# Causal attention's scores: two rows summed by TensorE, row 8's products moved to GpSimd, row 9's to VectorE

## The reference, cut to what matters

```
qkv = jnp.einsum('btd,ed->bte', x, Wqkv)
qkv = qkv.reshape(b, t, 3, H, DK).transpose(2, 0, 3, 1, 4)
q, k, v = (qkv[0], qkv[1], qkv[2])
scores = jnp.einsum('bhtd,bhsd->bhts', q, k) * SCALE
scores = jnp.clip(scores, -10.0, 10.0)
mask = jnp.triu(jnp.full((t, t), NEG, dtype=scores.dtype), k=1)
scores = scores + mask[None, None, :, :]
attn = jax.nn.softmax(scores, axis=-1)
out = jnp.einsum('bhts,bhsd->bhtd', attn, v)
out = out.transpose(0, 2, 1, 3).reshape(b, t, d)
return jnp.einsum('btd,ed->bte', out, Wout)
```

## Time and profile before

| | |
|---|---|
| median of 3 runs | 794.02 us (792.72 to 794.64) |
| the profiled execution | 794.07 us, its span 792.2 us, mean granted clock 0.941 |
| PE busy | 705.4 us (89% of the span) |
| DVE busy | 504.3 us (64%) |
| POOL busy | 417.3 us (53%) |
| ACT busy | 387.8 us (49%) |
| attention 1 and the low-rank layer | from about 690 us to the end |

### The profile page before, as it was taken

The page is one execution under the profiler, slowest core; times in us unless marked ns, Lnnn a source line. Parts: engine busy times, 40 slices in busy tenths (PEclk is TensorE's granted clock), DMA queues, the critical chain, the costliest instruction groups (busy, mean ns, idle before and its releaser), DMA issues.

```text
span 792.2 us, 13076 instructions
## 1 busy us (share of the span) xinstructions
PE 705.4 (89%) x4229; PEld 603.2 (76%) x4229; DVE 504.3 (64%) x1208; ACT 387.8 (49%) x982; POOL 417.3 (53%) x356
## 2 busy tenths in 40 slices
PE   3999999999999999999928629999999999596898
PEld 3889998888989887654727519999999999253786
DVE  3588877877877777768999551232223223578956
ACT  4586665766666655533135424444444444066241
POOL 5767867768586761549778021433343322136640
PEclk9999999999999999999859858999999999689799
DMA  7955233431443030000020089999999891300001
GB/s 235 259 146 158 71 115 105 116 114 61 116 116 112 5 107 1 1 0 1 0 108 1 0 310 345 326 326 313 343 318 333 322 335 52 140 1 0 2 1 67
DMA packets 47085, 108.59 MB, mean 137 GB/s; under 512 B 5048, under 2 KB 24748, under 8 KB 39596
## 3 DMA queue, kind: packets, MB, share of 16 engines
q1 hardware_dynamic: 44428, 100.68, 38.3%
q0 software_dynamic: 2592, 7.10, 2.5%
HBM read 101.58 MB, written 6.17 MB: 136 GB/s over the span
## 4 chain that ended last, share of the span: by engine, by line
PE 76%; DVE 14%; ACT 3%; DMA 2%; POOL 2%; issue 2%; SPq 0%; DVEq 0%; ACTq 0%; POOLq 0%
PE banks L1746 12%; PE banks L1754 12%; PE banks L292 9%; PE banks L294 9%; PE banks L293 9%; PE banks L299 6%; PE banks L305 4%; PE banks L1336 3%; DVE a_o L1615 2%; DVE a_prod L1224 2%; PE banks L1383 2%; DVE banks L1519 1%; PE banks L1310 1%; PE banks L1366 1%; DMA xraw<-in_x_rest 1%
## 5 line engine op out<-in xcount | busy, mean ns | idle before, releaser
L418 POOL TENSOR_TENSOR x_lo<-xraw,x_hi 128x512 fp32r<-128x512 f32 x81 | 106.2, 1311 | 77.1 <-ACT x_hi L412 76.9
L1836 ACT ACTIVATE hid<-banks,b 128x128 f32<-128x128 f32 x216 | 79.3, 367 | 110.4 <-PE banks L1746 110.4
L292 PE MATMUL banks<-wc_hi,x_hi 128*128 128x256 f32 x324 | 97.1, 300 | 13.4 <-POOL x_hi L421 9.7
L2003 DVE TENSOR_TENSOR res<-banks,xb 128x256 f32<-128x256 f32 x27 | 11.5, 424 | 127.5 <-PE banks L1754 127.5
L294 PE MATMUL banks<-wc_hi,x_lo 128*128 128x256 f32 x324 | 92.1, 284 | 0.0
L293 PE MATMUL banks<-wc_lo,x_hi 128*128 128x256 f32 x324 | 92.0, 284 | 0.0
L1874 POOL TENSOR_TENSOR y<-bve,mhalf 128x1 f32<-128x1 f32 x27 | 20.4, 754 | 105.2 <-DVE bve L2011 105.2
L454 DVE BATCH_NORM_STATS2 stats<-banks 128x6 f32<-128x256 f32 x81 | 34.6, 427 | 62.7 <-ACT pe_sb L448 62.0
L292 PEld LDWEIGHTS banks<-wc_hi,x_hi 128*128 128x128 f32 x324 | 62.3, 192 | 15.8 <-issue 10.2
L1746 PEld LDWEIGHTS banks<-xT,w_raw 128*128 128x128 f32 x448 | 67.9, 196 | 5.8 <-ACT xT L1824 0.9
L292 PE MATMUL banks<-wkv_hi,xg_hi 128*128 128x512 f32 x162 | 70.2, 433 | 0.5 <-DVE prod L546 0.3
(11 more groups left out here) (340 smaller groups left out, 1851.8 us busy)
## 6 DMA issues: line engine op xcount, KB each, us to landing
w_raw<-in_w SPq DMA_DIRECT2D x28, 1024.0 KB, 6.7
xraw<-in_x_main SPq DMA_DIRECT2D x26, 768.0 KB
w1more<-in_w SPq DMA_DIRECT2D x13, 1024.0 KB, 6.0
w2more<-in_w SPq DMA_DIRECT2D x13, 1024.0 KB, 8.8
xraw<-in_x_rest SPq DMA_DIRECT2D x48, 96.0 KB
xraw<-in_x_rest SPq DMA_DIRECT2D x26, 114.0 KB
yl<-y_rows SPq DMA_DIRECT2D x2, 1028.0 KB, 6.9
a_w<-in_qkv_w SPq DMA_DIRECT2D x2, 768.0 KB, 5.5
```

The costliest lines, as they stand in the source:

```text
L292: pe.matmul(dst, a[0], b[0], start=start, stop=False)
L418: pool.tensor_tensor(x_lo[:, i % RING_X, :], xraw[:, k, 0:KF].rearrange("p c b -> p (c b)"), x_hi[:, i % RING_X, 0:KF * P], ALU.subtract). ...
L1836: act.activation(hid[:, s % 2, fc, :], bank(fc % 2, 0, P), ACT.Gelu, bias=b1[:, bass.ds(e * FC + fc, 1)]).then_inc(sem("gelu_made"), 1)
```

## The change

In attention 1, POOL's rows become 1, 3, 5, 7 and 8, and DVE's 0, 2, 4, 6 and 9. The sums of rows 7 and 8 leave DVE: after the last value tile PE adds up each of them by 16 products with the identity, row 7 (128 columns) in bank 6 and row 8 (144 columns) in bank 5, in a new function with the same moving layout as `pe_sum_scores`. DVE then only clips them. DVE's order becomes: rows 0, 2, 4, 6 with the sums of rows 1, 3, 5 behind them, `softmax_half` 0, row 9 (product, sum, clip), the clips of rows 7 and 8, `softmax_half` 1. The first `project_o`, which writes bank 6, waits for all ten clips. The order of ACT's exponents ends with rows 9, 7, 8 instead of 8, 7, 9.

```diff
-            jobs = [("row", t + 1, t == 6 if layer == 0 else t % 2 == 1)]
+            jobs = [("row", t + 1, t == 6 if layer == 0 else t in POOL_ROWS)]
+        POOL_ROWS = (1, 3, 5, 7, 8)
+        SUMMED_ROWS = {7: 6, 8: 5}
...
+        def pe_sum_row(pe, t):
+
+            n, i = t + 1, [job[0] for job in pool_jobs(1)].index(t)
+            pe.wait_ge(sem("a_pool_prod_made"), len(pool_jobs(0)) + i + 1)
+            if SUMMED_ROWS[t] == 5:
+                pe.wait_ge(sem("a_qkv_made"), seen(1, "qkv_made", 2 * T))
+            by_channel = job_slot(1, i)[:, 0:n * C].rearrange("p (x d) -> p x d", d=D16)
+            for ch in range(D16):
+                last = pe.matmul(bank(SUMMED_ROWS[t], 0, n * H16), ident[:, :], by_channel[:, :, ch],
+                                 start=(ch == 0), stop=(ch == D16 - 1))
+            last.then_inc(sem("a_summed"), 1)
...
                     v_tile(pe, layer, t)
+                for t in SUMMED_ROWS:
+                    pe_sum_row(pe, t)
...
                 pe.wait_ge(sem("a_oT_made"), seen(layer, "oT_made", t + 1))
+                if layer == 1 and t == 0:
+                    pe.wait_ge(sem("a_s_made"), seen(1, "s_made", T))
...
-            return bank(7 if t < T - 1 else 4, 0, n * H16).rearrange("p (s h) -> p s h", s=n)
+            return bank(SUMMED_ROWS.get(t, 7 if t < T - 1 else 4), 0, n * H16).rearrange("p (s h) -> p s h", s=n)
-        SCORED = (0, 2, 1, 4, 3, 6, 5, 8, 7, 9)
+        SCORED = (0, 2, 1, 4, 3, 6, 5, 9, 7, 8)
...
-                for t in range(T + 1):
-                    if t < T:
-                        row_scores(dve, link, 1, t)
-                    if t == T - 2:
-                        softmax_half(dve, link, 1, 0)
+                for t in range(0, 8, 2):
+                    row_scores(dve, link, 1, t)
                     if t:
                         pool_sums(dve, link, 1, t - 1)
+                softmax_half(dve, link, 1, 0)
+                row_scores(dve, link, 1, T - 1)
+                for i, t in enumerate(SUMMED_ROWS):
+                    dve.wait_ge(sem("a_summed"), len(SUMS_ON_PE) + i + 1)
+                    clip(dve, link, 1, "row", t, t + 1)
                 softmax_half(dve, link, 1, 1)
```

## The result

The changed kernel took 798.0 us in its first five runs (797.17 to 798.17) beside 793.03 for the kernel before: a ratio of 1.0043, 95% interval 1.0024 to 1.0062, which is +3.4 us (+1.9 to +4.9). Twelve more runs beside 35 of the kernel before gave 796.40 and 795.08 us, 1.0022 (1.0008 to 1.0036), +1.7 us. The forecast was +1.34 us, 795.4, with a range up to 797.8. The first ratio on the 794.02 of before is 797.4, inside it near its end (the median itself, 798.0, is 0.2 above), the second is 795.8. The forecast's own, narrower range ended at 796.8: the first result is above it, the second inside. So the sign is right, and the first result is larger than the forecast.

What follows compares the result with a forecast made beforehand. From 725.12 us DVE alone was taken to bound the kernel for 13 us, then PE from 739.12. A 3.51 us later first `project_o` less 2.17 from the clock gave +1.34 us, 795.4 us; 8-in-10 range 793.6 to 797.8.

Steps and rivals of the forecast that it cites:

- The forecast's own, narrower range: Whole kernel: 794.2 to 796.8 us around the forecast of 795.4, which was given a chance of 0.70.
- DVE's way to the clip of row 9: Attention 1: `softmax_half` 0 ends at 727.0 us, then row 9's product, sum and clip end at 733.1.
- POOL's product of row 8: After row 7's product: starts about 725.5 us, takes 5.07, ends at 730.5, hidden behind PE's sums.
- The sums on PE: After the last value tile: 1.715 ns a column, row 7 7.02 us, row 8 7.90, ending at 741.29.
- The first projection: First `project_o`, behind the sums and two turns of 1.34 us: starts at 742.63 instead of 739.12, 3.51 us later.
- The clock: First `project_o` and `turn_o(2)` run at full instead of half clock: 1.63 and 0.54 us less, together 2.17.
- The slack at `turn_o(2)`: POOL's third row of weighted values is ready at 743.4 us, before `turn_o(2)` at 743.93: only 0.5 us slack.
- the rival of a bound behind PE: POOL or DVE becomes the bound behind PE, at most about 1 us more: 796.4 us; chance 0.08.
- the clock rivals: Half clock behind the sums (798.9 us, chance 0.09), or sums themselves at half clock and scaling (813 us, chance 0.02).
- That rival's time of 813 us: PE's sums run at half clock and scale with it: 14.9 us more, some 19 with the cold price; chance 0.02.
- The sum: Whole kernel: +3.51 us from the later first `project_o`, -2.17 from the clock, +1.34 us net.
- The reading of PE's idle time: Kernel before: PE does nothing in the 3.6 us after 726.4, comes back at 739 at half clock; work from 726 would warm it.

Runs made afterwards that it cites:

- price list: Kernel before plus 96 unused products behind the last value tile, operand steps 1, 2, 3, 4, 8, 16 floats; step 1 took 3.57 us, step 4 7.25.
- the contiguous kernel: Changed kernel, but POOL writes row 7 and 8 products so that PE reads contiguous columns; 789.76 us beside 794.64 for the kernel before, ratio 0.9932.
- the kernel with the busy PE: Kernel before plus 30 identity products behind the last value tile and 14 behind the second turn; 792.62 beside 794.64 us, ratio 0.9970.
- the kernel with row 8 alone: Changed kernel, but PE sums only row 8 and DVE sums row 7; 793.69 us beside 794.64 for the kernel before, ratio 0.9975.

## Why the prediction was right, step by step

- *DVE's way to the clip of row 9*: worked out 6.7 us after the value tile, measured 6.59 (734.76 - 728.17). The product and the sum were 2.81 and 2.83 us, for 2.82 and 2.84.
- *POOL's product of row 8*: forecast 4.1 us after the tile, measured 4.09, hidden as said.
- *The sums on PE*: 7.02 and 7.90 us forecast, 14.92 together, and 14.81 measured without a gap; 6.99 of it is row 7 by the kernel that sums row 7 alone, which leaves 7.82. This term carried the prediction. The earlier trace rows had the same form with 96 and 112 columns, and the price per column held at 128 and 144. The price list and the contiguous kernel show that it is the step of the operand.
- *The first projection*: forecast 16.26 us after the tile, measured 16.15; against before +3.40 instead of +3.51. That `turn_o(0)` and `turn_o(1)` are now in PE's way and ACT's exponent isn't was right; `project_o`'s new wait added nothing.
- *The clock*: 2.17 us forecast, 2.01 measured (4.81 to 2.80), and 1.91 in the kernel with the busy PE. The term was a little too large because the first `project_o`'s four records took 1.03 us at full clock (1.13 with the busy PE), and I had priced them as their successors, 0.87; what makes the first group longer isn't shown.
- *The slack at `turn_o(2)`*: it started right behind `project_o`, as in the forecast; the rival of a bound behind PE didn't come up. DVE had row 7's values ready at 755.99 us and PE turned them at 759.46, a cover of 3.5 where 5.4 less 2.1 were forecast. Nor did the clock rivals: the clock stayed at 1.00 behind the sums, and where at least two thirds of a sum ran at half clock, in the kernel with row 8 alone, the price went up by 5%. That rival's time of 813 us assumed a scaling that isn't there.
- *The sum*: +1.34 us forecast, +1.40 in the stage in each of two traces, +1.54 against the second trace of the kernel before. That it comes within 0.06 is partly luck: the delay was forecast 0.11 too long and the clock's gift 0.16 too large, and the two errors cancel.

The reading of PE's idle time was incomplete: between 726 and 739 us PE was not without work in the kernel before, but made the first two turns from 733.30 to 736.43 at half clock. This changes no term of the sum.

What the prediction mis-sized was the scatter. It took three runs of the kernel before, 1.9 us apart, for its spread; 35 runs are 5.7 us apart, and a part of that can arise far ahead of the stage, as the 1.5 us near 331 us show. The first five runs of the changed kernel lay together (797.17 to 798.17) where later only one run of twelve reached as high, and so the first ratio says +3.4 us where the second says +1.7; the interval of the latter holds the forecast. Why those five lay together stays open.

## What to carry to other kernels

Before reductions are given to PE as products with the identity, look at the step of the moving operand: a layout that the producing engine can write at no cost (0.05 us here) about halved the sums and turned the stage's +1.40 into -5.04 us. Count the freed engine's new wait, not only its busy time: DVE lost two sums of 2.57 and 2.21 us and gained a wait of 7.54. And a PE that goes idle ahead of a serial chain makes the chain's start dear; filling the gap was worth 1.9 us by itself.

## What the hardware showed that I had not expected

A strided sum hardly minds half the clock: 8.18 us, at least two thirds of them at 0.50, against 7.82 at 1.00 for 144 columns in steps of 16 floats, where the contiguous turns went from 1.52 to 3.13. The double price begins between steps of 2 and 4 floats (3.63, 5.54, 7.25 us), and a step of 16 is slightly cheaper than one of 8 (6.97 against 7.46), in one trace. GpSimd's strided write of the same data cost nothing that could be seen (9.67 against 9.62 us).
